# A graph network on one core: the edge attributes' share of the message's first layer, made in the second attention instead of in the last edge stage

## The reference

```python
h = jnp.maximum(_layernorm(x), 0.0)
# _L1_gnn_ref
h = jnp.concatenate([x[row], edge_attr], axis=1)      # (12500, 256)
h = jax.nn.relu(h @ W1a + b1a) @ W1b + b1b            # W1a (256, 256)
s = jax.ops.segment_sum(h, col, num_segments=x.shape[0])
agg = s / jnp.maximum(cnt, 1.0)[:, None]
h2 = jnp.concatenate([x, agg, u[batch]], axis=1)
return jax.nn.relu(h2 @ W2a + b2a) @ W2b + b2b
```

## Time and profile before

| | |
|---|---|
| median of 3 runs | 2521.88 us (2516.39 to 2528.07) |
| profiled execution, device time | 2527.11 us |
| its span, first to last instruction | 2525.3 us |
| PE busy | 2013.4 us (80%) |
| DVE / ACT / POOL busy | 69% / 54% / 51% |
| mean granted clock of PE | 0.92 |
| moved by DMA | 526.75 MB, 209 GB/s on average |
| second attention, first sweep | about 1224 to 1399 us |
| last edge stage | about 2129 us to the end |

### The profile page before, as it was taken

The page is one execution under the profiler, slowest core; times in us unless marked ns, Lnnn a source line. Parts: engine busy times, 40 slices in busy tenths (PEclk is TensorE's granted clock), DMA queues, the critical chain, the costliest instruction groups (busy, mean ns, idle before and its releaser), DMA issues. The chain is left out here.

```text
span 2525.3 us, 38804 instructions
## 1 busy us (share of the span) xinstructions
PE 2013.4 (80%) x7514; PEld 1160.2 (46%) x7514; DVE 1733.3 (69%) x5020; ACT 1371.6 (54%) x2609; POOL 1290.4 (51%) x1119
## 2 busy tenths in 40 slices
PE   0898889879795777778366796499999995799997
PEld 0444444434232444444133232377777774466665
DVE  3899999965797777778422798477777773454552
ACT  0888888862121666666122221477667763556552
POOL 4645554418830333333587000677777763577773
PEclk9999999989797999999677798699999998899999
DMA  4778888859232999999544132999999993434440
GB/s 142 227 245 252 251 256 256 254 178 271 63 92 74 342 360 359 361 368 367 159 122 103 50 90 66 262 293 302 303 305 300 303 290 117 104 95 115 110 111 21
DMA packets 316448, 526.75 MB, mean 209 GB/s; under 512 B 87187, under 2 KB 189472, under 8 KB 316199
## 3 DMA queue, kind: packets, MB, share of 16 engines
q1 hardware_dynamic: 266100, 492.30, 61.5%
q0 software_dynamic: 46400, 33.03, 6.2%
q10 hardware_dynamic: 3824, 0.13, 0.1%
HBM read 304.11 MB, written 221.80 MB: 208 GB/s over the span
## 5 line engine op out<-in xcount | busy, mean ns | idle before, releaser
L476 POOL DMA_INDIRECT first_x<-in_x,first_index x200 | 254.5, 1272 | 230.1 <-ACT first_xn L339 140.8
L339 ACT ACTIVATE first_xn<-first_x,first_nb,first_rstd 125x128 f32<-125x128 f32 x600 | 245.4, 485 | 63.8 <-DVE first_nb L525 63.8
L795 POOL DMA_INDIRECT second_entry<-node_map,second_si x100 | 128.0, 1280 | 258.8 <-DVE second_src_row L808 221.0
L1086 PE MATMUL last_psH<-last_g,W2a 128*128 128x500 f32 x400 | 197.5, 618 | 31.9 <-DVE last_hid L1048 31.9
L868 PE MATMUL second_psZ<-second_h,gate_h 128*128 128x500 f32 x200 | 108.5, 624 | 112.8 <-DVE second_y L820 85.8
L1095 PE MATMUL last_psO<-W2b,last_hid 128*125 128x128 f32 x1600 | 193.3, 275 | 0.0
L1119 POOL DMA_INDIRECT elast_x<-x_rows,elast_si x100 | 138.6, 1386 | 99.8 <-issue 96.6
L1095 PEld LDWEIGHTS last_psO<-W2b,last_hid 128*125 128x125 f32 x1600 | 185.3, 190 | 0.9 <-issue 0.9
L585 PE MATMUL first_psZ<-first_h,gate_h 128*128 128x500 f32 x250 | 131.4, 607 | 47.6 <-DVE first_y L546 46.1
L339 ACT ACTIVATE last_xn<-last_x,last_nb,last_rstd 125x128 f32<-125x128 f32 x400 | 164.0, 486 | 0.1
L577 PE MATMUL first_psW<-first_h,W_in 128*128 128x500 f32 x300 | 157.6, 608 | 0.0
(11 more groups left out here) (260 smaller groups left out, 5326.1 us busy)
## 6 DMA issues: line engine op xcount, KB each, us to landing
hT<-first_h SPq DMA_DIRECT2D x100, 250.0 KB, 3.4
yT<-first_y SPq DMA_DIRECT2D x100, 250.0 KB, 3.5
second_yin<-yT SPq DMA_DIRECT2D x50, 500.0 KB
second_hin<-hT SPq DMA_DIRECT2D x50, 500.0 KB
yT<-second_y SPq DMA_DIRECT2D x50, 500.0 KB
last_yin<-yT SPq DMA_DIRECT2D x50, 500.0 KB
first_x<-in_x SPq DMA_DIRECT2D x100, 224.0 KB
h_rows<-second_rows SPq DMA_DIRECT2D x50, 448.0 KB
```

Source lines behind the costliest of these rows:

```text
L339: last = act.activation(xn[:, j], x[:, j], ACT.Relu, bias=nb[:, j:j + 1], scale=rstd[:, j:j + 1])
L476: pool.indirect_dma_start(x[:, to % X, j], None, a["x"], bass.IndirectOffsetOnAxis(index[:, end, r % 2, j:j + 1], 0), bounds_check=NODES - ...
L795: pool.indirect_dma_start(entry[:, q], None, scratch.node_map, bass.IndirectOffsetOnAxis(si[:, q], 0), bounds_check=NODES - 1, oob_is_err= ...
L1086: last = pe.matmul(psH[h][:, 0:CH], w.W2a[:, 0, h * 128:(h + 1) * 128], g[:, q % 2], start=True, stop=True)
```

## The change

The lower half of `W1a` is applied to the attributes in the first sweep of the second attention. Per chunk k: SP loads the attributes there (`load_attr`, two buffers, held until PE has turned chunk k - 2), PE turns them (`turn_attr`), ACT copies them to one buffer `eT`, PE makes the two halves one after the other in one PSUM bank (`attr_part`), ACT takes each out with its bias `b1a` (`attr_out`), and SP stores both, five turns later, to new tables `ehT[0]`, `ehT[1]` in DRAM. The buffers are ones that this sweep did not use: `eT` is the tile `wt`, `eh` the tiles `o` and `sig`, `ea` lies in `yn`, the PSUM tiles are banks 6 and 7.

In `edge_last` the attributes' load, transposes, copy and two matmuls a chunk are gone. SP loads the two stored halves instead (two DMAs of 128 partitions), DVE adds them to `psH` into a new tile `pre`, and ACT applies relu to both halves (`halves`); DVE's `half` is gone.

Four transposes and two matmuls are gone from the turn. The diff, cut to its core:

```diff
+            eT, eh = wt, (o, sig)
+            ea = yn[0:TILE].rearrange("p u e -> p (u e)")[:, 0:2 * TILES * D].rearrange("p (s j f) -> p s j f", s=2, j=TILES)
+            ea_loaded, eh_stored = ph.loaded("ea_loaded", 2), ph.stored("eh_stored", 2)
+            psA, psP = bank[6], bank[7]
...
+                def load_attr(k):
+                    hold(sp, ph.seen, m.eaT, made(k - 2))
+                    sp.dma_start(flat(ea, k % 2), rows_of(a["edge_attr_128"], k * CH)).then_inc(ea_loaded[k % 2], 16)
+
+                def store_attr(k):
+                    hold(sp, ph.seen, m.eh1, made(k))
+                    for h in range(2):
+                        sp.dma_start(cols_of(scratch.ehT[h], k * CH), eh[h][:, k % 2]).then_inc(eh_stored[k % 2], 16)
...
-                steps(C, [(0, load_index), (0, load), (0, load_weights_wide)])
+                steps(C, [(0, load_index), (0, load), (0, load_weights_wide)] + [(0, load_attr), (5, store_attr)] * l)
...
+                def turn_attr(k):
+                    pe.wait_ge(ea_loaded[k % 2], 16 * (k // 2 + 1))
+                    pe.wait_ge(m.eT, made(k - 1))
+                    to_T(pe, psA, ea[:, k % 2], w.ident, m.eaT)
+
+                def attr_part(h):
+
+                    def step(k):
+                        pe.wait_ge(m.eT, made(k))
+                        pe.wait_ge(m.eh1 if h == 0 else m.eh0, made(k - 1 + h))
+                        pe.matmul(psP[:, 0:CH], w.W1a[:, 1, h * 128:(h + 1) * 128], eT[:], start=True, stop=True).then_inc(m.attr1 if h else m.attr0, 1)
+                    return step
...
-                steps(C, [(0, turn)] * l + [(l, query_key), (l + 1, score)])
+                if l == 1:
+                    steps(C, [(0, turn), (0, turn_attr), (1, attr_part(0)), (1, query_key), (1, attr_part(1)), (2, score)])
+                else:
+                    steps(C, [(0, query_key), (1, score)])
...
+                def attr_T(k):
+                    act.wait_ge(m.eaT, made(k))
+                    act.wait_ge(m.attr1, made(k - 1))
+                    act.activation(by_edge(eT[:]), by_tile(psA), ACT.Identity).then_inc(m.eT, 1)
+
+                def attr_out(h):
+
+                    def step(k):
+                        act.wait_ge(m.attr1 if h else m.attr0, made(k))
+                        act.wait_ge(eh_stored[k % 2], 32 * (k // 2) + 16)
+                        act.activation(eh[h][:, k % 2], psP[:, 0:CH], ACT.Identity, bias=w.b1a[:, h:h + 1]).then_inc(m.eh1 if h else m.eh0, 1)
+                    return step
...
-                steps(C, [(0, source)] * l + [(l, query)])
+                if l == 1:
+                    steps(C, [(0, source), (1, attr_out(0)), (1, query), (1, attr_out(1)), (0, attr_T)])
+                else:
+                    steps(C, [(0, query)])
...
-                    hold(sp, ph.seen, m.eaT, made(k - U))
-                    sp.dma_start(flat(ea, q), rows_of(a["edge_attr_128"], k * CH)).then_inc(ea_loaded[q], 16)
+                    hold(sp, ph.seen, m.pre1, made(k - U))
+                    for h in range(2):
+                        sp.dma_start(eh[:, q, h], cols_of(scratch.ehT[h], k * CH)).then_inc(eh_loaded[q], 16)
...
-                def half(k, q, r):
+                def add_attr(k, q, r):
                     dve.wait_ge(m.hidden, made(k))
-                    dve.wait_ge(m.psm, made(k - 2))
-                    dve.tensor_scalar(hid[:, q % 2, 1], psH[1][:, 0:CH], w.b1a[:, 1:2], 0.0, ALU.add, ALU.max).then_inc(m.hid1, 1)
+                    dve.wait_ge(eh_loaded[q], 32 * r + 32)
+                    dve.wait_ge(m.hid0, made(k - 2))
+                    dve.tensor_tensor(pre[:, q % 2, 0], psH[0][:, 0:CH], eh[:, q, 0], ALU.add).then_inc(m.pre0, 1)
+                    dve.wait_ge(m.hid1, made(k - 2))
+                    dve.tensor_tensor(pre[:, q % 2, 1], psH[1][:, 0:CH], eh[:, q, 1], ALU.add).then_inc(m.pre1, 1)
...
-                pipeline(dve, ECHUNK, U, [(2, bias), (0, stats), (0, aggr), (6, output), (3, add_bias), (4, total), (5, half2), (3, half)], peel=U)
+                pipeline(dve, ECHUNK, U, [(2, bias), (0, stats), (0, aggr), (6, output), (3, add_bias), (4, total), (5, half2), (3, add_attr)], peel=U)
...
-                    pe.wait_ge(m.eT, made(k - 1))
+                    pe.wait_ge(m.g, made(k - 1))
...
-                def turn_attr(k, q, r):
-                    pe.wait_ge(ea_loaded[q], 16 * r + 16)
+                def hidden(k, q, r):
                     pe.wait_ge(m.g, made(k))
-                    for j in range(TILES):
-                        last = pe.transpose(psT[0][:, j * TILE:(j + 1) * TILE], ea[:, q, j], w.ident[0:TILE, 0:TILE])
-                    last.then_inc(m.eaT, 1)
-
-                def hidden(k, q, r):
-                    pe.wait_ge(m.eT, made(k))
-                    pe.wait_ge(m.hid0, made(k - 1))
-                    pe.wait_ge(m.hid1, made(k - 1))
+                    pe.wait_ge(m.pre0, made(k - 1))
+                    pe.wait_ge(m.pre1, made(k - 1))
                     for h in range(2):
-                        pe.matmul(psH[h][:, 0:CH], w.W1a[:, 0, h * 128:(h + 1) * 128], g[:, q, 1], start=True, stop=False)
-                        last = pe.matmul(psH[h][:, 0:CH], w.W1a[:, 1, h * 128:(h + 1) * 128], eT[:, q % 2], start=False, stop=True)
+                        last = pe.matmul(psH[h][:, 0:CH], w.W1a[:, 0, h * 128:(h + 1) * 128], g[:, q, 1], start=True, stop=True)
                     last.then_inc(m.hidden, 1)
 
...
-                pipeline(pe, ECHUNK, U, [(3, turn), (6, output), (4, message), (3, turn_attr), (5, hidden2), (3, hidden)])
+                pipeline(pe, ECHUNK, U, [(3, turn), (6, output), (4, message), (5, hidden2), (3, hidden)])
...
-                def make_eT(k, q, r):
-                    act.wait_ge(m.eaT, made(k))
-                    act.wait_ge(m.hidden, made(k - 2))
-                    act.activation(by_edge(eT[:, q % 2]), by_tile(psT[0]), ACT.Identity).then_inc(m.eT, 1)
-
-                def half(k, q, r):
-                    act.wait_ge(m.hidden, made(k))
+                def halves(k, q, r):
+                    act.wait_ge(m.pre0, made(k))
                     act.wait_ge(m.psm, made(k - 2))
-                    act.activation(hid[:, q % 2, 0], psH[0][:, 0:CH], ACT.Relu, bias=w.b1a[:, 0:1]).then_inc(m.hid0, 1)
+                    act.activation(hid[:, q % 2, 0], pre[:, q % 2, 0], ACT.Relu).then_inc(m.hid0, 1)
+                    act.wait_ge(m.pre1, made(k))
+                    act.activation(hid[:, q % 2, 1], pre[:, q % 2, 1], ACT.Relu).then_inc(m.hid1, 1)
...
-                pipeline(act, ECHUNK, U, [(3, make_g), (2, make_xn), (4, make_msg), (3, make_eT), (5, half2), (3, half), (1, deviation)])
+                pipeline(act, ECHUNK, U, [(3, make_g), (2, make_xn), (4, make_msg), (5, half2), (3, halves), (1, deviation)])
```

More of the change, by code:

```diff
@@ L1192, in attention @@
             rows = ph.sb("rows", [TILE, U, TILES, D])
+            eT, eh = wt, (o, sig)
+            ea = yn[0:TILE].rearrange("p u e -> p (u e)")[:, 0:2 * TILES * D].rearrange("p (s j f) -> p s j f", s=2, j=TILES)
+            ea_loaded, eh_stored = ph.loaded("ea_loaded", 2), ph.stored("eh_stored", 2)
+            psA, psP = bank[6], bank[7]
         yn_stored = ph.stored("yn_stored", U)
-        names = "xT hs qk qs kj prod score weight spread v vs pv o xz gated sig dx gx y yn ystats"
+        names = "eaT eT eh0 eh1 attr0 attr1 xT hs qk qs kj prod score weight spread v vs pv o xz gated sig dx gx y yn ystats"
         m = Group(**{n: ph.stage(n + "_made") for n in names.split()})
@@ L1252, in _ @@
                     sp.wait_ge(moved[q], 16 * TILES * len(range(q, C, U)))
+                if l == 1:
+                    for s in range(2):
+                        sp.wait_ge(eh_stored[s], 16 + 32 * len(range(s, C, 2)))
             @block.tensor
@@ L1490, in edge_last @@
         xb = ph.sb("xb", [TILE, U, TILES, D])
-        ea = ph.sb("ea", [TILE, U, TILES, D])
+        eh = ph.sb("eh", [128, U, 2, CH])
         xn = ph.sb("xn", [TILE, 2, N2, D])
@@ L1507, in edge_last @@
         psM, psO = ph.ps("psM"), ph.ps("psO")
-        idx_loaded, ends_loaded, x_loaded, ea_loaded, run_loaded = (
-            ph.loaded(n, U) for n in ("idx_loaded", "ends_loaded", "x_loaded", "ea_loaded", "run_loaded"))
+        idx_loaded, ends_loaded, x_loaded, eh_loaded, run_loaded = (
+            ph.loaded(n, U) for n in ("idx_loaded", "ends_loaded", "x_loaded", "eh_loaded", "run_loaded"))
         moved, placed = ph.loaded("moved", U), ph.loaded("placed", U)
-        names = ("xb stats aggr_seen aggr sd rstd nb xn xT g eaT eT hid0 hid1 hidden psm msg tot mean "
+        names = ("xb stats aggr_seen aggr sd rstd nb xn xT g pre0 pre1 hid0 hid1 hidden psm msg tot mean "
                  "hidden2 hid20 hid21 o_ps o init")
@@ L1720, in program @@
         hdT=dram("hdT", (128, EDGES)), hsT=dram("hsT", (128, EDGES)), ydT=dram("ydT", (128, EDGES)),
-        ywT=dram("ywT", (128, EDGES)))
```

(1 more changed line is left out.)

4 lines of the change are left out of this document (2 added, 2 removed).

## The result

The changed kernel takes 2642.82 us (median of 4 runs, 2636.94 to 2648.87); beside it the kernel before took 2519.14. The ratio is 1.048, with a 95% interval of 1.046 to 1.051: 124 us slower, where I had forecast no change and a range up to 2538. The profiled execution of the changed kernel took 2648.87 us.

What follows compares the result with a forecast made beforehand. It took the last edge stage as bound by a loop through SP's load burst and the second attention's sweep by POOL; -6.3 - 15 + 16 + 3 = -2.3 gave a median of 2519.6 us, range 2500 to 2538.

Steps and rivals of the forecast that it cites:

- the +19 forecast: Second attention's first sweep: +16 us for added DMA and +3 us for a longer drain.
- rival C: Second attention's sweep: in-order chain through one buffer and one PSUM bank sets the turn as clock falls; 2544 us, chance 0.10.
- SP's queue: Second attention's sweep: indices behind the waiting queue allow 6.3 us a turn, so they bite only together with the DMA bound.
- DMA in the sweep, +16: Second attention's sweep: added transfers, with 125-row loads on five engines, raise the turn from 6.33 to 7.0 us; +16 us.
- rival B: Second attention's sweep hides its added DMA and POOL keeps 6.33 us a chunk; 2503 us, chance 0.22.
- A: The forecast itself: sweep and last stage move as summed and cancel; 2519.6 us, from 2508 to 2532, chance 0.52.
- The drain, +3: End of the second attention's sweep: after the last gather PE still has attribute work before the last score; +3 us.
- The last stage, -15 and -6.3: Last edge stage: shorter load burst saves 0.75 us over 20 turns, -15 us; less PE work in the drain, -6.3 us.
- Rival D: Last edge stage: burst no shorter because 256 KB more pays back the relief, only the drain gains; 2535 us, chance 0.16.
- The floor of 12.8 us: Last edge stage: POOL's gathers allow no turn shorter than 12.8 us.
- 8.8 us from x's issue to the statistics: Last edge stage: time from issue of the x load to DVE's statistics falls to 8.8 us from 9.5.
- ACT's and DVE's rearranged work in the last stage: Last edge stage: ACT loses a copy, DVE gets some 0.6 us more, covered by idling and PE work; no cost.

Runs made afterwards that it cites:

- e1: Changed kernel with its attribute stores issued four SP turns late instead of five; 2533.16 us, ratio 1.0048 to the kernel before.
- e5: Changed kernel with store lag 4 instead of 5 and the second attention's index loads issued three SP turns earlier; 2513.88 us, ratio 0.9974.
- e6: e5 with the sweep's attribute load cut into two transfers of 112 and 13 rows; 2510.78 us, ratio 0.9965.
- e11: e5 with the store lag at 3 in place of 4, index loads still three turns early; 2516.70 us.
- e4: Changed kernel with the second attention's attribute loads left out after the first two chunks, holds and stores kept; 2566.78 us.
- e7: Kernel before, with the last edge stage's x and attribute loads each cut into 112 and 13 rows; 2520.85 us, ratio 0.9979.
- e8: Changed kernel, lag 5 and two buffers kept, with the second attention's attribute load cut into 112 and 13 rows; 2595.20 us.

## Why the prediction was wrong

**The step that failed.** In the terms of the second attention I wrote: "The buffers that are stored are next written in the second sweep, behind the softmax; at nothing." The buffers are written again two chunks later, in the same sweep, by `attr_out`, which waits for their store. I had priced SP's holds as far as they delay the indices, and never followed the added wait on `eh_stored` back to the SP turn that issues the store. Worked out by the same means as the rest it would have been there: 7 us for issue and landing, and about 6 us from ACT's output to the next transposes on PE, serial, near 13 us a turn from the third chunk on until SP has nothing more to load. It measured 12.97 us a turn (13.65 in the one shown), +121.7 in the gathers and, with the drain, +139.6 against the +19 forecast. None of my rivals had this mechanism, so the range could not hold it; rival C was on its side only by its sign.

**SP's queue**, "it only bites together with the DMA bound". Wrong too, but small: with lag 4 the gathers took 23.7 us more (e1), and moving the indices forward recovered it (e5) with the DMA share at 0.81, so the late indices needed no DMA bound.

**DMA in the sweep, +16.** Too high. With lag 4 and early indices, the gathers take 161.8 us instead of 160.7 (e5), and cutting the 125-row load changes nothing (e6). This term belonged to rival B: its 6.33 us a chunk came true. The share of 0.81 in e5 is what was forecast for A (in the changed kernel it is 0.41); I was wrong to add the five engines' shares up to a turn. By the Trainium skill (DMA: Bandwidth & Descriptors, the part on where 436 GB/s comes from) 358 GB/s would have left room for it. The outcome agrees, but at a measured mean of 237 GB/s it does not test the rule.

**The drain, +3.** Too low: 12.8 to 21.7 us in e5, so +9. There PE, whose shortest turn is 5.8 us, is some microseconds behind when the gathers end, which I had not counted: its last transposes of gathered rows start at 1389.10, 7.1 us after the last gather did, where before it is 3.4 (1388.01 and 1384.6). From there the last group of scores starts 10.3 us later, at 1399.37; before, it is 8.2 (1396.22). ACT's remaining wait for stores is not the reason: e6 and e11 have none, and drains of 22.3 and 22.5 us. The scores of e5:

```profile
1389.10 0.59 PE L346 MATMUL att_bank<-ident,att_rows 125*128 125x125 f32 x4
...
1394.04 1.00 PE L1303 MATMUL att_bank<-att_prod,heads 128*128 128x500 f32 x2
...
1399.37 2.10 PE L1303 MATMUL att_bank<-att_prod,heads 128*128 128x500 f32 x4
```

**Rival C, the chain at half clock.** Not what sets the turn. In e5 the granted clock is 1.00 in the window shown, and PE runs whole turns in 5.8 us (1389.10 - 1383.31), beside the 5.9 worked out. In the changed kernel the clock stayed low, 0.76 where the kernel before has 0.80; that adds some 1.7 us to a turn, by the estimate at e4, and the wait for the store is the rest of the loss.

**The last stage, -15 and -6.3.** Right in kind, a little large. Turn 13.07 us (13.0 forecast): 20 x 0.68 = -13.6. Last statistics to the end: 80.5 to 75.6, -4.9. Together -18.5, and -19.1 for the whole stage, against -21.3. Rival D is out. That the burst, by its 125-row loads, set this stage in the kernel before is what the trace of e7 says. In the changed kernel it is POOL, with 0.2 us of slack a turn. The floor of 12.8 us was worked out rightly, (90.3 + 77.0 + 38.4) / 16 = 12.9 by the rows above, and the stage runs on it; that 13.0 came out as the turn is so in part luck, for I had the burst still setting it. "8.8 us from x's issue to the statistics" was too low and the fall was right: over 18 turns in the middle it is 9.05 us on average where the kernel before has 9.83, and it varies, 9.43 from the issue at 2483.15 and 2504.91 - 2496.57 = 8.34 from the next.

```profile
2483.15 0.26 SPq L1572 DMA_DIRECT2D elast_x<-x_rows  x1
...
2496.57 0.24 SPq L1572 DMA_DIRECT2D elast_x<-x_rows  x1
```

**ACT's and DVE's rearranged work in the last stage, "at nothing".** Holds for the turn. PE now waits at times and is at full clock less (0.91 in the window, 1.00 before; busy 92% where 85% was forecast), and POOL's rows leave no room for it to have set the turn.

With the failed step mended and the indices moved (e5), the forecast's own terms measure +1 (for +16), +9 (for +3) and -19 (for -21): about -9, and the times of e5 say -6.6 (-12.6 to -0.5). The idea of the change was good for some 7 us; the lag of five in one list cost 110 (e1).

## What to carry to other kernels

For every buffer that a DMA empties, find the turn in which the queue's program *issues* that DMA, what is held ahead of it there, and who waits for it: the buffers must cover the lag of the issue and the landing, not only the landing. Of a wait added by a change, follow it to its release before pricing it at nothing. And small loads that feed the bounding engine (indices) go ahead of any hold in the same program: here that was worth 20 us for one number in a list.

## What the runs showed of the hardware

When a transfer lands depends on the shape of a transfer issued shortly ahead of it on the same queue. From the issue of the second half's store to ACT's release it is 6.15 us on average behind a 250 KB load of 125 rows (changed kernel), 3.74 behind the same bytes as 112 and 13 rows (e8), and 3.57 behind no load (e4), over 20 waits each. The Trainium skill (DMA: Bandwidth & Descriptors, the section on why a DMA increments its semaphore by 16) has a transfer use the largest number of engines, up to 16, that divides its slowest dimension; that gives 5 for 125, 16 for 112 and 13 for 13. These three numbers agree with it, and so does the trace of e7's last stage.

With more work, PE ran at a higher clock. In the sweep before, the granted clock was 0.80 with PE busy for 64% of the time; in e5, with the attribute part added and POOL at the same pace, it is 1.00 with PE busy for 84%. In the changed kernel, where PE waits in every turn, it is 0.76 with PE busy for 59%.
